# ACT sums all three interaction layers, stores go out from ACT's queue, and transposes move ahead of the wait for x2

## The reference, cut to what matters

```python
e = stack([tbl_f[ids[:, f]] for f in range(32)])          # x0: B = 1024, M = 32, D = 16
xk = x0 = e
for W in (W0, W1, W2):                                     # (32, 32, 64), (32, 64, 64), (32, 64, 64)
    xk = relu(einsum('bmd,bhd,mhk->bkd', x0, xk, W))       # (B, 64, 16)
    outs.append(sum(xk, axis=2))                           # the sum over d
z = concatenate(outs, axis=1)                              # (B, 192)
h = maximum(concatenate([z, dense_ctx], 1) @ W_top1 + b_top1, 0)
h = maximum(h @ W_top2 + b_top2, 0)
y = h @ W_top3
```

## Time and profile before

| | us |
|---|---|
| median of 3 runs | 660.86 (655.26 to 666.55) |
| the profiled execution | 658.72 |
| its span, first to last instruction | 656.9 |
| mean granted TensorE clock | 0.98 of full speed |

### The profile page before, as it was taken

How to read it: one execution, slowest core, us unless ns; L and a number is a source line. 1 busy time by engine, 2 the same in 40 slices (tenths; PEclk the granted TensorE clock), 3 DMA queues, 4 the chain that set the end, 5 groups by cost and what they waited for, 6 DMA issues and landing times.

```text
span 656.9 us, 7762 instructions
## 1 busy us (share of the span) xinstructions
PE 569.1 (87%) x2620; PEld 205.7 (31%) x2620; DVE 560.9 (85%) x245; ACT 321.3 (49%) x1333; POOL 458.2 (70%) x353
## 2 busy tenths in 40 slices
PE   0379698979999898989898989999998989897996
PEld 0145232323233333323232323333333323232332
DVE  0379799989899999999999999999999999989300
ACT  0224446434736556564736363736556565606121
POOL 6776578878598787888887979788888883444000
PEclk9989799979989999999999999999999999999999
DMA  3858785758577685858484867777685848444000
GB/s 98 271 174 320 289 335 210 275 188 306 232 277 293 240 330 194 303 220 329 176 326 184 310 245 278 293 278 292 238 331 192 342 182 339 163 177 89 1 0 0
DMA packets 29586, 153.03 MB, mean 233 GB/s; under 512 B 7487, under 2 KB 17579, under 8 KB 20971
## 3 DMA queue, kind: packets, MB, share of 16 engines
q1 hardware_dynamic: 19659, 149.11, 59.0%
q0 software_dynamic: 8192, 2.11, 2.5%
q10 hardware_dynamic: 1696, 1.32, 0.7%
HBM read 147.60 MB, written 4.92 MB: 232 GB/s over the span
## 4 chain that ended last, share of the span: by engine, by line
PE 44%; DVE 28%; issue 11%; DMA 9%; ACT 4%; POOL 3%; SPq 0%; POOLq 0%; DVEq 0%
PE acc L587 39%; DVE prod L427 25%; DMA spread<-x_scratch 4%; ACT x L490 4%; DMA x_scratch<-xt 2%; POOL rows L376 2%; PE x L660 2%; PE x L649 1%; DVE z L440 1%; POOL prod_pool L389 1%; DMA x_scratch_half<-xt 1%; DVE xt L416 1%; DMA rows<-table,ids_sb 1%; PE x L666 1%; PE x L653 0%
## 5 line engine op out<-in xcount | busy, mean ns | idle before, releaser
L427 DVE TENSOR_TENSOR prod<-spread,x 128x4096 f32<-128x4096 f32 (+3 forms) x190 | 532.5, 2862 | 36.6 <-issue 11.8
L587 PE MATMUL acc<-prod,w 128*64 128x512 f32 (+1 forms) x2076 | 449.6, 581 | 79.8 <-DVE prod L427 79.8
L376 POOL DMA_INDIRECT rows<-table,ids_sb x256 | 243.2, 950 | 76.8 <-issue 70.0
L587 PEld LDWEIGHTS acc<-prod,w 128*64 128x64 f32 x2076 | 160.4, 141 | 358.7 <-issue 320.2
L389 POOL TENSOR_TENSOR prod_pool<-spread,x_pool 128x1024 f32<-128x1024 f32 (+1 forms) x93 | 214.8, 2341 | 67.6 <-ACT x_pool L490 67.4
L490 ACT ACTIVATE x<-acc 64x512 f32<-64x512 f32 (+1 forms) x136 | 74.1, 545 | 88.4 <-PE acc L587 87.1
L506 ACT ACTIVATE relu_out<-acc 128x512 f32<-128x512 f32 (+1 forms) x51 | 29.2, 573 | 150.5 <-PE acc L587 149.6
L498 ACT ACTIVATE relu_out<-relu_out 128x16 f32<-128x16 f32 x480 | 95.3, 200 | 0.5
L587 PE MATMUL acc<-prod_pool,w 128*64 128x512 f32 (+1 forms) x372 | 89.8, 585 | 0.0
L498 ACT ACTIVATION_READ_ACCUMULATOR relu_out<-relu_out 128x1 f32 x480 | 89.8, 187 | 0.0
L490 ACT ACTIVATE x_pool<-acc 64x512 f32<-64x512 f32 (+1 forms) x136 | 77.1, 567 | 2.0
(11 more groups left out here) (21 smaller groups left out, 26.0 us busy)
## 6 DMA issues: line engine op xcount, KB each, us to landing
spread<-x_scratch SPq DMA_DIRECT2D x60, 2048.0 KB, 8.5
first<-x_scratch SPq DMA_DIRECT2D x15, 512.0 KB, 3.7
spread<-x_scratch_half SPq DMA_DIRECT2D x7, 1024.0 KB, 6.2
rows<-table,ids_sb POOLq DMA_INDIRECT x256
x_scratch<-xt SPq DMA_DIRECT2D x15, 256.0 KB
w<-w ACTq DMA_DIRECT2D x2, 512.0 KB, 5.3
spread<-x_scratch_half SPq DMA_DIRECT2D x4, 256.0 KB, 3.9
spread<-wt SPq DMA_DIRECT2D x2, 384.0 KB, 4.7
```

The costliest lines, as they stand in the source:

```text
L376: nc.gpsimd.indirect_dma_start(rows[u % 2][:, j * D:(j + 1) * D], None, table, bass.IndirectOffsetOnAxis(ap=index, axis=0)).then_inc(gathe ...
L427: nc.vector.tensor_tensor(prod[:, at:at + count, 0:n], tiles(u, t, count), x[:, 0:n].rearrange("p (a n) -> p a n", a=1).to_broadcast([P, c ...
L587: last = nc.tensor.matmul(parts(to[K * blk:K * blk + K, 0:n]), w, side(moving[:, 0:2 * n], blk), start=start, stop=stop)
```

## The change

- ACT takes all sums. `sum_kept` sums layers 1 and 3 straight out of the PSUM accumulator (ReLU and sum in one activation per sample), and the accumulator is free only when all samples are summed. Layer 2 is kept in SBUF as before and summed later (`sum_2`), behind the sums of layer 1 of the next unit. Only the sum of layer 3 of the last unit stays on DVE.
- From unit 1 on, the transpose of unit u+2 stands ahead of DVE's wait for x2 of unit u.
- The stores are issued from ACT's queue: after x1 for units 1 and 2, after layer 2's kept copy for later units; of unit 0 the second of the two.
- POOL issues 9 gathers of unit u+2 and the first 2 of unit u+3 (`EARLY`) after layer 2's products, and 5 more after layer 3's (`AHEAD` is 7).
- The last step of layer 3, four tiles, becomes two of two. Copies of x for POOL are left out in units where POOL makes no tiles.

```diff
-AHEAD = 5
+EARLY = 2
+AHEAD = 7
 def steps_of(layer, u):
-    return (0, 4), (4, second), (8, 4), (12, 4)
+    return (0, 4), (4, second), (8, 4), (12, 2), (14, 2)
...
         @block.sync
             for u in range(LAST):
-                sp.wait_ge(turned, u + 2)
-                store(sp, u + 1)
                 load_first(u + 1)
...
         @block.gpsimd
                 products(u, 2)
-                if u + 2 < UNITS:
-                    gather(u + 2, slice(AHEAD, fields(u + 2)))
+                gather(u + 2, slice(AHEAD, None))
+                gather(u + 3, slice(0, EARLY))
                 products(u, 3)
-                if u + 3 < UNITS:
-                    gather(u + 3, slice(0, AHEAD))
+                gather(u + 3, slice(EARLY, AHEAD))
...
         @block.vector
                 layer_1(u + 1)
-                sum_d(u, 0)
+                if 0 < u and u + 2 < UNITS:
+                    turn(u + 2)
                 dve.wait_ge(x_ready[1], u + 1)
                 if u + 1 < LAST:
                     for i in range(len(steps_of(3, u))):
-                        if i == (2 if u == 0 else 3) and u + 2 < UNITS:
-                            turn(u + 2)
+                        if i == 2 and u == 0:
+                            turn(2)
                         multiply(3, u, i, x2)
-                        if i == 2:
-                            sum_d(u, 1)
...
         @block.scalar
+            def sum_kept(u, layer, src):
+                if u:
+                    act.wait_ge(summed[layer], u)
+                n = width(u) // 2
+                per_b = src[:, 0:n].rearrange("p (c b e) -> p b c e", c=4, e=D // 4)
+                to = relu_out[layer][:, 0:n].rearrange("p (b c e) -> p b c e", c=4, e=D // 4)
+                for b in range(samples(u)):
+                    last = nc.scalar.activation(to[:, b, :, :], per_b[:, b, :, :], ACT.Relu,
+                                                accum_out=z[:, layer, z_at(u) + b:z_at(u) + b + 1])
+                last.then_inc(summed[layer], 1)
+            def stores(u):
+                act.wait_ge(turned, u + 1)
+                store(act, u)
+                store_wrapped(act, u)
             def after_1(u):
                 spread_out(u, x1, src).then_inc(x_ready[0], 1)
+                if u < 2:
+                    stores(u + 1)
...
-                keep(u, 0, src)
+                sum_kept(u, 0, src)
             def after_2(u):
...
+                nc.scalar.activation(relu_out[1][:, 0:n], src[:, 0:n], ACT.Relu).then_inc(relu_2_ready, 1)
+                if 0 < u and u + 2 < UNITS:
+                    stores(u + 2)
...
                 after_2(u)
                 after_1(u + 1)
+                sum_2(u)
                 if u + 1 < LAST:
                     after_3(u)
-                    sum_3(u)
...
         @block.tensor
-                    pe.wait_ge(relu_ready[before[0] - 1], before[1] + 1)
+                    pe.wait_ge((summed[0], relu_2_ready, summed[2])[before[0] - 1], before[1] + 1)
```

More of the change, by code:

```diff
@@ L30 @@
 POOL_SLOTS = 4
-AHEAD = 5
-MIDDLE = 11
+EARLY = 2
+AHEAD = 7
 def half(u):
@@ L79, in order_of @@
                 ("step", 3), ("step", 4), ("step", 5)]
-    return [("step", 0), ("step", 1), ("pool", 0), ("pool", 1), ("step", 2), ("pool", 2), ("step", 3)]
+    return [("step", 0), ("step", 1), ("pool", 0), ("pool", 1), ("step", 2), ("pool", 2), ("step", 3),
+            ("step", 4)]
 CUT = 2
-CUT_ORDER = ([("step", 0), ("step", 1), ("pool", 0), ("pool", 1), ("pool", 2)], [("step", 2), ("step", 3)])
+CUT_ORDER = ([("step", 0), ("step", 1), ("pool", 0), ("pool", 1), ("pool", 2)], [("step", 2), ("step", 3), ("step", 4)])
 def sequence():
@@ L147, in made, with pool_units @@
     return PLACES[layer, u, i % len(steps_of(layer, u))][0] + 1
+def pool_units(layer, u):
+    return sum(1 for v in range(u + 1) if pool_tiles(layer, v))
 def used(layer, u):
@@ L235, in build @@
         x_pool_ready = [sem(f"x{l + 1}_pool_ready") for l in range(2)]
-        relu_ready = [sem(f"relu_ready{l}") for l in range(3)]
+        relu_2_ready, relu_last_ready = sem("relu_2_ready"), sem("relu_last_ready")
         summed = [sem(f"summed{l}") for l in range(3)]
@@ L278, in store, with store_wrapped @@
             engine.dma_start(to, src.to_broadcast([P, 2, n])).then_inc(scratch_in[u % 2], 16)
+        def store_wrapped(engine, u):
+            n = width(u) // 4
             to = scratch(u, 2 * M)
@@ L341, in _ @@
                 if u >= 1:
-                    sp.wait_ge(prod_ready, made(3, u - 1, 3))
+                    sp.wait_ge(prod_ready, made(3, u - 1))
                 load_group(u + 1, 1)
@@ L370, in gather @@
             def gather(u, part):
+                if u >= UNITS:
+                    return
                 if part.start == 0 and u >= 2:
@@ L382, in products @@
                 if pool_tiles(layer, u):
-                    pool.wait_ge(x_pool_ready[layer - 2], u + 1)
+                    pool.wait_ge(x_pool_ready[layer - 2], pool_units(layer, u))
                 for i, t in enumerate(pool_tiles(layer, u)):
@@ L435, in layer_1 @@
                     multiply(1, u, i, x0)
[L437 to L442, removed]
             dve.wait_ge(ids0_in, 16)
@@ L473, in _ @@
                 multiply(2, LAST, i, x1)
-            sum_d(LAST, 0)
             for i in range(CUT, len(steps_of(3, LAST - 1))):
@@ L479, in _ @@
                 multiply(3, LAST, i, x2_of(LAST))
-                if i == 1:
-                    sum_d(LAST, 1)
-            sum_d(LAST, 2)
+            dve.wait_ge(relu_last_ready, 1)
+            nc.vector.tensor_reduce(z[:, 2, z_at(LAST):COLS],
+                                    relu_out[2][:, :].rearrange("p (c b e) -> p b c e", c=4, e=D // 4),
+                                    axis=mybir.AxisListType.XY, op=ALU.add).then_inc(summed[2], 1)
         @block.scalar
@@ L505, in keep, with sum_2 @@
                 n = width(u) // 2
-                nc.scalar.activation(relu_out[layer][:, 0:n], src[:, 0:n], ACT.Relu).then_inc(relu_ready[layer], 1)
+                per_b = src[:, 0:n].rearrange("p (c b e) -> p b c e", c=4, e=D // 4)
[4 more added lines that the diff above has]
+                last.then_inc(summed[layer], 1)
+            def sum_2(u):
+                act.wait_ge(relu_2_ready, u + 1)
+                kept = relu_out[1][:, 0:width(u) // 2].rearrange("p (c b e) -> p b c e", c=4, e=D // 4)
+                for b in range(samples(u)):
+                    last = nc.scalar.activation(kept[:, b, :, :], kept[:, b, :, :], ACT.Copy,
+                                                accum_out=z[:, 1, z_at(u) + b:z_at(u) + b + 1])
+                last.then_inc(summed[1], 1)
             def base_tile(u):
@@ L524, in after_1 @@
                 spread_out(u, x1, src).then_inc(x_ready[0], 1)
-                spread_out(u, x1_pool, src).then_inc(x_pool_ready[0], 1)
-                keep(u, 0, src)
+                if u < 2:
+                    stores(u + 1)
+                if pool_tiles(2, u):
+                    spread_out(u, x1_pool, src).then_inc(x_pool_ready[0], 1)
+                sum_kept(u, 0, src)
             def after_2(u):
@@ L533, in after_2 @@
                     squares(1)
-                spread_out(u, x2_pool_of(u), src).then_inc(x_pool_ready[1], 1)
-                keep(u, 1, src)
+                if pool_tiles(3, u):
+                    spread_out(u, x2_pool_of(u), src).then_inc(x_pool_ready[1], 1)
+                if u:
+                    act.wait_ge(summed[1], u)
+                n = width(u) // 2
+                nc.scalar.activation(relu_out[1][:, 0:n], src[:, 0:n], ACT.Relu).then_inc(relu_2_ready, 1)
+                if 0 < u and u + 2 < UNITS:
+                    stores(u + 2)
             def after_3(u):
                 act.wait_ge(prod_free, used(3, u))
-                keep(u, 2, acc[BANKS[3, u][0]])
+                src = acc[BANKS[3, u][0]]
+                if u < LAST:
+                    sum_kept(u, 2, src)
+                else:
+                    act.wait_ge(summed[2], LAST)
+                    nc.scalar.activation(relu_out[2][:, :], src[:, :], ACT.Relu).then_inc(relu_last_ready, 1)
             act.dma_start(w_1[:, :, :], w1a).then_inc(consts_in, 16)
@@ L551, in _ @@
             nc.scalar.activation(warm[:, :], w_sq[0:1, 0:1], ACT.Relu)
+            act.wait_ge(turned, 1)
+            store_wrapped(act, 0)
             base_tile(0)
@@ L560, in _ @@
                 after_1(u + 1)
+                sum_2(u)
                 if u + 1 < LAST:
                     after_3(u)
-                    sum_3(u)
             after_2(LAST)
             after_3(LAST - 1)
-            sum_3(LAST - 1)
+            sum_2(LAST)
             after_3(LAST)
```

1 line of the change is left out of this document (removed).

## The result

| | before | after |
|---|---|---|
| median of 20 runs each | 665.32 us | 669.08 us (664.31 to 672.97) |
| ratio to before, 95% interval | | 1.0112, 1.0086 to 1.0137 |
| the profiled execution | 658.72 us | 670.74 us |
| its span | 656.9 us | 668.9 us |
| its mean granted TensorE clock | 0.980 | 0.963 |

The kernel became slower by 1.1%, where I forecast 0.7% faster. The step is under the 2% that I named as the limit of telling, but the interval excludes no change. The ratio takes only executions within 1.5% of the fastest of their kernel, which leaves out 11 of the 20 of the kernel before; the medians of all 20, which the table gives, are 0.6% apart. The result lies inside my wide range (646 to 690) and outside the forecast's own (648 to 661).

The account below looks back on a forecast made before the run. DVE, with 0.66 us to spare per period, bounds the kernel, but PE's own loop takes over at once. 658.7 - 6 + 1.7 - 0.4 - 0.6 = 653.4 us profiled, median 656; forecast 648 to 661, wide range 646 to 690.

Parts of the forecast that it names:

- the start: Up to 145 us: earlier stores on ACT's queue shorten DVE's base-tile waits, -6 us, ends -10.5 and +2.
- the loop: Ten steady periods: gather wait +1.7 us over nine periods, the tenth gives 0.4 back; +1.3 in all.
- the tail: Last two units: one removed sum stood before the last layer 3's first product, -0.6 us (at most 1.8).
- the gathers: Transpose ahead of x2's wait: last gather issued 36.23 us after layer 2's end, landing 1.42; period 35.37 us.
- Rival B: Gathers land late, 4.21 us, before the transposes: loop loses 14.3 us instead of 1.7, median 668; chance 0.10.
- then 16 tiles of layer 3 and 16 of layer 2 follow, 32 x 0.871 = 27.86: PE's loop, from its start on layer 3 to layer 2's end: 32 tiles at 0.871 us, 27.86 us.
- I cost it at nothing, hidden behind PE: ACT's sums in the steady loop: 32.7 us of work, 2.5 less than the period, accumulators freed in time; cost nothing.
- DVE's idle of the earlier trace, up to 145 us, to fall by half: Sign of being right: DVE's 10.5 us in four base-tile waits up to 145 us falls by half.
- Rival A: ACT becomes the bound: a PSUM pair takes 0.28 us, ACT's loop 37.8 us, median 688; chance 0.31.
- my lower bound of 0.19: ACT's activation and accumulator read per sample from PSUM: 0.19 us if the read covers the activation, up to 0.39.
- The x2 copies: Four PSUM-to-PSUM activations on ACT without overlap (4 x 0.57 in 2.31 us), taken as evidence for ACT becoming the bound.
- rival C: Transpose doesn't wait, start recovers all: PE's 34.80 us holds in ten periods, -10.5 at start, median 646; chance 0.12.

Follow-up runs that it names:

- The filler run: Changed kernel plus two contractions (8 matmuls) on PE ahead of layer 3 into the accumulator layer 3 overwrites: 658.06 us, ratio 0.9921.
- the control: Kernel before the change plus one filling contraction (four matmuls) ahead of layer 3: 664.88 us, ratio 1.0012.

## Why the prediction was wrong, and where it was right

Against the profiled execution my terms add up to -5.3 us, and the spans differ by +12.0. Of these 17.3 us the start missed by 11.5 (+5.5 for -6), the loop by 6.8 (+8.1 for +1.3) and the tail by -1.0. In the order of the prediction:

- **Right: the gathers.** I put the last gather's issue 36.23 us after layer 2's end on PE, and the landing at 1.42 us. Measured from 361.74, where the chain's PE run ends: 397.89 - 361.74 = 36.15, and 399.32 - 397.89 = 1.43. Rival B (4.21 us) falls.
- **Wrong, the first failing step: "then 16 tiles of layer 3 and 16 of layer 2 follow, 32 x 0.871 = 27.86".** The count is right, the duration holds only at full clock. I took the rate from rows in which PE's pauses were 1.28 and 1.02, and then lengthened the pause ahead of layer 3 without asking what the clock does after it. From PE's start to layer 2's end it took 29.40 us (the chain's row at 404.43). Two periods should have been 69.31 + 1.43 = 70.74, and were 433.85 - 361.74 = 72.11: 1.4 more, nearly the whole price of one half-clock stretch (6.21 - 4.51 = 1.70). So a period is 35.99 (359.87 / 10) where I had 35.37, and the loop lost 8.1 us where I had 1.3. The filler run shows the cause: waits no shorter, full clock, 35.33 per period. I priced the gather wait rightly; the step that failed is that the matmuls behind the pause would keep their full-clock price.
- **Wrong, the second: the accumulator.** "I cost it at nothing, hidden behind PE" was worked out for the steady loop, and there it holds. At unit 2 the layer that must cover ACT's sums is layer 3 of a half unit, on PE for about 7 us (83.0 to 90.1 in the changed kernel's trace), and PE waits 3.20 us; at unit 16, in the tail, 1.64 us. With the half clock that follows, this was worth 5.4 us between the two medians and 4.7 us in the traces, all of it at the start.
- **Wrong, the third: -6 at the start.** This is the largest miss in microseconds. I expected DVE's idle of the earlier trace rows, up to 145 us, to fall by half. The same group reads:

```profile
DVE prod L437 <- issue: 13.0, 2, 8.0
```

  Two waits in place of four, but longer. The longest, 8.0 us, ends the chain turn, store, load for unit 2: the store is issued right after the transpose in either kernel (50.65 before, 50.59 after), so ACT's queue had nothing to win there. Of the 5.5 us some 4 seem to be this execution's alone: the store's second part took 8.66 us to land here (5.93 before), and in the five experiments with the same queue DVE's products of that unit start at 64.4 to 68.0 us instead of 71.9. From there to layer 3 of unit 5 the two kernels take nearly the same, 147.4 us and before 146.9.
- **Right: ACT.** Rival A falls. 32 pairs out of PSUM take 5.40 us, 0.169 each, below my lower bound of 0.19, and ACT is busy 287.63 / 10 = 28.8 us per period where I had 32.7 (of that 1.0 for two stores, which busy time does not count; by the row it should have been 2 x 0.59 = 1.18, and nothing turns on it). The x2 copies were the wrong likeness. The Trainium skill (ScalarE: Activation LUTs, section What ACT_TABLE_LOAD costs) says that neighbouring activations overlap by about 93 ns. By that rule the pair stayed near 0.2 us, on the side where ACT keeps its slack; the row here is lower still.
- **Half right: rival C.** PE's loop of 34.80 us exists: 34.86 was measured, once neither wait nor clock stood against it. That the ordering as changed would not reach it, because the gathers end after the period, was right too.
- **The tail:** -1.6 for -0.6, inside its bounds.

What stays open is when the clock falls. A pause of 1.88 us was followed by full clock at 368.65 in the changed kernel, one of 1.54 by half clock in the run with earlier gathers, one of 1.97 in the control. In the loop of the run with earlier gathers three of eight pauses of 1.53 or 1.54 us were followed by half clock, and neither of the two of 1.88. The length of one pause does not decide by itself, and the runs here don't show what does. Nor do they show how often the clock falls in the loop of the kernel before in its other executions, so how much of the 3.8 us between the medians the clock makes is argued from the traces, not measured.

## What to carry to other kernels

A wait ahead of PE can have two prices, as here: the wait and the clock after it; look for rows in which the same matmuls take longer, before blaming the wait. When work is moved so that two short pauses of PE become one longer one, cost the matmuls behind it at either level of the clock, or fill or split so that PE starts sooner. And a cover that is worked out in the steady loop must be worked out again at the first and the last full unit, where the neighbouring unit is shorter or missing.

## What was not expected of the hardware

- In a loop in which PE is busy 92% (332.28 of 359.87 us), a pause of 1.88 us was followed by half clock in two cases of six and one of 2.7 us in four of four: 20 matmuls then took 6.21 us instead of 4.51, and each stretch at the lower level in this loop lasted 3.4 us.
- An activation with its accumulator read was cheaper out of PSUM (0.169 us a pair, with ReLU) than out of SBUF (0.20, a copy).
- The time that the same store took to land differed by more between executions than between queues: from its second issue to the first load behind it 5.2 to 8.7 us on ACT's queue, 5.9 to 7.7 on SP's, over the ten profiles.
